# Two-layer transformer-like block on one core: diagonal attention tiles packed two to a bank, and the turned output blocks handled by ScalarE and GpSimd

## What is computed

```python
# first attention: scores plus a slope times the distance
scores = einsum('bhqd,bhkd->bhqk', Q, K) / sqrt(16) + slope * (k - q)
attn   = softmax(where(k <= q, scores, -inf))
out    = einsum('bhqk,bhkd->bqhd', attn, V)
# second attention: rotated q and k, 4 key heads shared by 16 query heads
scores = where(k <= q, einsum('bqhd,bkhd->bhqk', q, k) * scale, min)
out    = einsum('bhqk,bhkd->bqhd', softmax(scores), v)
```

## Time and profile before

| | us |
|---|---|
| median of 3 runs (2500.06 to 2501.35) | 2500.09 |
| the profiled execution | 2502.25 |
| its span, first to last instruction | 2500.4 |
| TensorE busy | 2322.5 (93%) |
| VectorE busy | 1916.5 (77%) |
| ScalarE busy | 1514.3 (61%) |
| GpSimd busy | 583.8 (23%) |

### The profile page before, as it was taken

The page is one execution under the profiler, slowest core; times in us unless marked ns, Lnnn a source line. Parts: engine busy times, 40 slices in busy tenths (PEclk is TensorE's granted clock), DMA queues, the critical chain, the costliest instruction groups (busy, mean ns, idle before and its releaser), DMA issues. The chain is left out here.

```text
span 2500.4 us, 49324 instructions
## 1 busy us (share of the span) xinstructions
PE 2322.5 (93%) x16370; PEld 1302.1 (52%) x16371; DVE 1916.5 (77%) x5054; ACT 1514.3 (61%) x3292; POOL 583.8 (23%) x845
## 2 busy tenths in 40 slices
PE   3599989999999999999999999999998874999997
PEld 2355555444444444444444444444444653788886
DVE  7777658999999999999999999999981663333332
ACT  3133323688888888888888888887886551222221
POOL 6412101121111111211211211111010366333323
PEclk8799996999999999999999999999999986999999
DMA  4167776453443443322332332331032973344443
GB/s 159 64 188 216 209 202 90 82 110 76 77 82 80 75 81 81 61 55 60 62 58 57 61 60 54 61 67 50 25 91 86 301 269 146 71 76 76 78 76 70
DMA packets 168152, 246.51 MB, mean 99 GB/s; under 512 B 52120, under 2 KB 124968, under 8 KB 162100
## 3 DMA queue, kind: packets, MB, share of 16 engines
q0 software_dynamic: 38304, 112.51, 23.9%
q1 hardware_dynamic: 124596, 121.03, 16.5%
q10 hardware_dynamic: 5044, 10.32, 1.4%
HBM read 120.38 MB, written 122.36 MB: 97 GB/s over the span
## 5 line engine op out<-in xcount | busy, mean ns | idle before, releaser
L1404 ACT ACTIVATE a_p<-banks 128x512 f32<-128x512 f32 (+3 forms) x2560 | 1169.6, 542 | 282.1 <-PE banks L1307 174.7
L1451 DVE TENSOR_REDUCE a_mx<-banks 128x1 f32<-128x512 f32 x1536 | 962.3, 683 | 23.8 <-PE banks L1298 21.4
L1368 PE MATMUL banks<-a_p,a_v 128*32 128x512 f32 (+3 forms) x5120 | 601.6, 547 | 1.7 <-ACT a_o L1422 1.7
L1447 DVE CUSTOM_DVE_ANT_0 a_masked<-banks,a_later 128x128 bf16<-128x128 f32 (+3 forms) x1024 | 460.1, 486 | 42.6 <-PE banks L1298 28.8
L1298 PE MATMUL banks<-a_k,a_q 48*128 48x512 f32 (+7 forms) x1600 | 454.5, 428 | 2.9 <-DVE a_mx L1451 1.0
L1307 PE MATMUL banks<-a_q,a_k 50*128 50x512 f32 (+7 forms) x1600 | 433.2, 407 | 1.1
L1298 PEld LDWEIGHTS banks<-a_k,a_q 52*128 52x128 f32 (+1 forms) x1600 | 216.4, 185 | 205.7 <-DVE a_mx L1451 132.5
L1307 PEld LDWEIGHTS banks<-a_q,a_k 54*128 54x128 f32 (+1 forms) x1600 | 216.6, 185 | 137.2 <-ACT a_p L1404 38.3
L1298 PE MATMUL banks<-a_k,q 48*128 48x512 f32 (+7 forms) x896 | 255.0, 434 | 3.1 <-DMA a_k<-aug_rows 1.3
L1307 PE MATMUL banks<-q,a_k 50*128 50x512 f32 (+7 forms) x896 | 236.7, 414 | 0.7 <-DVE a_mx L1447 0.2
L2141 ACT ACTIVATE e_hT<-banks 128x256 fp32r<-128x256 f32 x72 | 27.6, 383 | 309.2 <-PE banks L2067 278.9
(11 more groups left out here) (267 smaller groups left out, 2629.1 us busy)
## 6 DMA issues: line engine op xcount, KB each, us to landing
expert_rows<-a_zeros POOLq DMA_DIRECT2D x132, 258.0 KB, 5.3
a_k<-ka_parts POOLq DMA_DIRECT2D x42, 256.0 KB, 6.3
e_x<-expert_rows SPq DMA_DIRECT2D x72, 129.0 KB, 2.9
expert_rows<-e_y SPq DMA_DIRECT2D x72, 128.0 KB, 2.1
qa_parts<-m_part SPq DMA_DIRECT2D x16, 512.0 KB
ka_parts<-m_part SPq DMA_DIRECT2D x16, 512.0 KB, 4.9
va_tiles<-m_va SPq DMA_DIRECT2D x8, 1024.0 KB, 4.7
qb_parts<-m_part SPq DMA_DIRECT2D x16, 512.0 KB, 4.7
```

Source lines behind the costliest of these rows:

```text
L1368: ins = pe.matmul(ps_o[VW * h:VW * h + VW, c0:QB], v_op[o][:, kt, hk * VW:hk * VW + VW], prob[:, (t * NSC + n * GH + h) % NPB, c0:QB], sta ...
L1404: nc.scalar.activation(prob[:, (t * NSC + n) % NPB, c0:QB], ps[bank][:, c0:QB], ACT.Exp, scale=SCALE).then_inc(s_ex, 1)
L1447: ins = v.tensor_tensor_reduce(masked[:, 2 * (DIAGONAL.index(m) % 2) + j, 0:w], ps[bank][:, 0:w], later[:, WIDE - w:WIDE], 1.0, MASKED, AL ...
L1451: ins = v.tensor_reduce(top, ps[bank][:, 0:w], AX.X, ALU.max)
```

## The change

Diagonal tiles that don't fill a bank share one: of each pair of heads, the tile of 384 columns with that of 128 (`ends`), and the two pairs' tiles of 256 (`middle`). The number and width of the products stays, but for the mask's, which now treat both tiles of a bank at once (moving operand 64 or 2 x 64 columns); VectorE still does one masked maximum for each tile, ScalarE one exponential for each bank. A step has 136 banks of maxima, 136 of scores and 280 in all. A score group of the value product is now a full key tile, `widest`, `ends` (eight products of two records each) or `middle`; there are 36 of them for 40.

The maxima of query blocks 0 and 1 no longer pass through `mx` and the last reduction (DIRECT = 2): block 0's masked maximum is written straight to `row_top`, block 1's takes the maximum of its first key block in `mx` as its starting value through a pointer. `row_top` has two buffers. Blocks 2 and 3 are as before. The scratch `masked` has 2 buffers for 4.

A turned output block is copied by ScalarE from the bank to `t_sb` (272 columns), VectorE takes the reciprocal from there, and GpSimd multiplies (`weigh`, 128 x 256 with the factor broadcast). Both strings are new, with d for ScalarE's copy and a new letter e for reciprocal, product and store. In `ORDER` (312 letters for 348) the e stands directly behind its d for output block 3, 34 places behind it for blocks 0 and 2, and 68 for block 1. In `FIRST_ORDER` the first score of query blocks 0 to 3 stands 3, 3, 10 and 6 places behind the w of its row maxima, for 19, 21, 28 and 29 before. LEAD is 42 (of 68), SLEAD 4. TensorE now waits for the mask `later` too before its first product.

```diff
+def score_groups():
...
+        widest = [[(p, 4 * qb, 0, QB, 0)] for p in range(PAIRS)]
+        ends = [[(p, 4 * qb + 1, P, 3 * P, P), (p, 4 * qb + 3, 3 * P, P, 0)] for p in range(PAIRS)]
+        middle = [[(p, 4 * qb + 2, 2 * P, 2 * P, 2 * P * p) for p in range(PAIRS)]]
...
+            def weigh(t, n):
+
+                pool.wait_ge(s_rc, t * NQB + (n + 1))
+                pool.wait_ge(s_os[n % 2], t * (NQB // 2 * 16) + (n // 2 * 16 + 16))
+                nc.gpsimd.tensor_tensor(o_row[n % 2][:, :, :].rearrange("p j (h c) -> p j h c", h=GH),
+                                        t_sb[n % 2][:, :, :, 0:HD],
+                                        rec[n % 2][:, :, :].unsqueeze(3).to_broadcast([P, 4, GH, HD]), ALU.mult
+                                        ).then_inc(s_or, 1)
...
-            pe.wait_ge(M["s_masks"], 48)
+            pe.wait_ge(M["s_masks"], 64)
...
-                        ins[j] = pe.matmul(outs[j][:, HALF * n:HALF * (n + 1)], steps[n][half, :], fill[half, :],
+                        blocks = outs[j][:, lo:lo + len(at) * apart].rearrange("p (b c) -> p b c", c=apart)
+                        ins[j] = pe.matmul(blocks[:, :, HALF * n:HALF * (n + 1)], steps[n][half, :],
+                                           fill[half, :].unsqueeze(1).to_broadcast([HALF, len(at), HALF]),
...
+                    elif what == "turn copied":
+                        turned = ps[BANKS[t]["turn", n]].rearrange("p (j h c) -> p j h c", j=4, h=GH)
+                        act.wait_ge(s_tt, t * NQB + (n + 1 + TT0))
+                        if t > 0 or n >= 2:
+
+                            act.wait_ge(s_or, t * NQB + (n - 1))
+                        nc.scalar.activation(t_sb[n % 2][:, :, :, :], turned[:, :, :, 0:HD + 1], ACT.Copy).then_inc(s_te, 1)
...
+                for p, qt, k0, w, col in tiles:
+                    top = mx[:, j, p, qt, k0 // WIDE:k0 // WIDE + 1]
+                    if diagonal:
+                        least = mx[:, j, p, qt, 0:1] if qb == 1 else MASKED
+                        if qb < DIRECT:
+                            top = row_top[:, qb % 2, j * PAIRS + p, qt % 4:qt % 4 + 1]
+                        ins = v.tensor_tensor_reduce(masked[:, j, col:col + w], ps[bank][:, col:col + w],
+                                                     later[:, WIDE - w:WIDE], 1.0, least, ALU.add, ALU.max, top)
+                    else:
+                        ins = v.tensor_reduce(top, ps[bank][:, :], AX.X, ALU.max)
...
-                if m == LAST_MAX[qb] and j == 1:
+                if m == LAST_MAX[qb] and j == 1 and qb >= DIRECT:
...
-                        ch.did(v.reciprocal(rec[:, :, :], turned[:, :, :, HD]))
-                        ch.settle()
...
-                        v.tensor_tensor(o_row[n % 2][:, :, :].rearrange("p j (h c) -> p j h c", h=GH),
-                                        turned[:, :, :, 0:HD],
-                                        rec[:, :, :].unsqueeze(3).to_broadcast([P, 4, GH, HD]), ALU.mult
-                                        ).then_inc(s_te, 1)
+                        v.reciprocal(rec[n % 2][:, :, :], t_sb[n % 2][:, :, :, HD]).then_inc(s_rc, 1)
```

More of the change, by code:

```diff
@@ L934 @@
 NPB = 20
[L935 to L960, removed]
+LEAD = 42
+SLEAD = 4
+def score_groups():
+    groups = []
+    for qb in range(NQB):
+        full = [[[(p, kt, 0, QB, 0)] for p in range(PAIRS)] for kt in range(4 * qb)]
+        widest = [[(p, 4 * qb, 0, QB, 0)] for p in range(PAIRS)]
+        ends = [[(p, 4 * qb + 1, P, 3 * P, P), (p, 4 * qb + 3, 3 * P, P, 0)] for p in range(PAIRS)]
+        middle = [[(p, 4 * qb + 2, 2 * P, 2 * P, 2 * P * p) for p in range(PAIRS)]]
+        between = [ends, middle, widest] if qb else [widest, ends, middle]
+        for d, diagonal in enumerate(between):
+            groups += [(qb, False, pairs) for pairs in full[len(full) * d // 3:len(full) * (d + 1) // 3]]
+            groups.append((qb, True, diagonal))
+    return groups
@@ new lines, in max_banks, with full, ends, widest @@
+def max_banks():
+    banks = []
+    for qb in range(NQB):
+        first = 4 * qb * P
+        def full(p, i):
+            return [(qb, False, [(p, 4 * qb + i, k0, WIDE, 0)]) for k0 in range(0, first, WIDE)]
+        def ends(p):
+            return [(qb, True, [(p, 4 * qb + 2, first, 3 * P, P), (p, 4 * qb, first, P, 0)])]
+        def widest(p):
+            return [(qb, True, [(p, 4 * qb + 3, first, WIDE, 0)])]
+        middle = [(qb, True, [(p, 4 * qb + 1, first, 2 * P, 2 * P * p) for p in range(PAIRS)])]
+        banks += full(0, 0) + full(0, 2) + ends(0) + full(0, 1) + full(0, 3) + widest(0)
+        banks += full(1, 1) + middle + full(1, 0) + full(1, 2) + ends(1) + full(1, 3) + widest(1)
+    return banks
@@ new lines @@
+GROUPS, MAXES = score_groups(), max_banks()
+SCORES = [(qb, diagonal, tiles) for qb, diagonal, pairs in GROUPS for tiles in pairs]
+NSP, NMX, NGR = len(SCORES), len(MAXES), len(GROUPS)
+SFIRST = [sum(len(pairs) for of, _, pairs in GROUPS if of < qb) for qb in range(NQB)]
+VFIRST = [sum(of < qb for of, _, _ in GROUPS) for qb in range(NQB)]
+RUN = [g for g in range(NGR) for _ in GROUPS[g][2]]
+PAIR0 = [RUN.index(g) for g in range(NGR)]
+KEYED = [min(m for m in range(NMX) if MAXES[m][2][0][2] >= k0) for k0 in (WIDE, 2 * WIDE)]
@@ L1049, in attention @@
         o_sb = [sb(f"a_o{i}", [P, QB]) for i in range(2)]
-        rec = sb("a_rec", [P, 4, GH])
+        t_sb = [sb(f"a_turned{i}", [P, 4, GH, HD + 1]) for i in range(2)]
+        rec = [sb(f"a_rec{i}", [P, 4, GH]) for i in range(2)]
         o_row = [sb(f"a_orow{i}", [P, 4, GH * HD]) for i in range(2)]
@@ L1242, in step @@
                         parts(t, h)
+                    elif what == "inverse":
+                        weigh(t, h)
                     elif h % 2:
@@ L1266, in _, with mask @@
             pe.sem_inc(s_rt, RT0)
-            pe.sem_inc(s_pv, PV0)
-            pe.wait_ge(M["s_masks"], 48)
-            def mask(outs, steps):
+            pe.wait_ge(M["s_masks"], 64)
+            def mask(outs, tiles, steps):
+                at = [col for _, _, _, _, col in tiles]
+                lo, apart = min(at), abs(at[-1] - at[0]) or P
                 ins = [None, None]
@@ L1339, in step @@
                     elif what == "score":
[L1340 to L1341 removed]
+                        qb, _, tiles = SCORES[n // 2 % NSP]
+                        if n % 2 == 0 and n // 2 % NSP == SFIRST[qb]:
                             pe.wait_ge(s_mr[qb], (t + n // NSC + 1) * NMR)
@@ L1349, in step @@
                             score_half(t + n // NSC, n + 1, second)
-                            at = columns(qb, kt)
-                            for ins in mask([ps[b][:, at:at + P] for b in (bank, second)], after_q):
+                            for ins in mask([ps[b] for b in (bank, second)], tiles, after_q):
                                 ins.then_inc(s_sc, 1)
```

163 lines of the change are left out of this document (83 added, 80 removed).

## The result

The kernel became slower: 2514.59 us, median of 20 executions (2496.63 to 2520.97), against 2502.03 of 20 of the kernel before; ratio 1.0036, interval 1.0023 to 1.005. The forecast was 2453, range 2420 to 2478. The profiled execution took 2516.19 us, with a span of 2514.4.

What follows compares the result with a forecast made beforehand. VectorE, slightly ahead of TensorE and tied to it by 7 banks, was taken as the bound. Steps 1 to 14 at -3.3 us each gave -46, step 0 -1, last step and tail 0: -47, to 2453 us, range 2420 to 2478.

Steps and rivals of the forecast that it cites:

- The step that failed: GpSimd in steps 1 to 14: 3 us of multiplies a step, covered by 2 us to the next queued work; cost nothing.
- packing, row tops, banks, narrow tiles: Steps 1 to 14: direct row tops save 0.7 us a step, fewer banks and fuller tiles 1.2.
- pointer: Block 1's 16 masked maxima a step take their start from SBUF: 0 to 0.06 us each, 0.45 taken.
- turned blocks: Product and a wait leave VectorE, a reciprocal stays: four blocks save 2.3 us a step in steps 1 to 14.
- VectorE's wait for ScalarE's copy: Block 3's reciprocal directly follows its copy, so VectorE waits: +0.45 us a step, 0.2 to 2.
- the tie of the ring: VectorE and TensorE, nearly full, share 7 banks: 4.8 of 93.0 us a step lost, 1.2 recovered, bounds 0 and 3.5.
- The wait for `later`: Ahead of TensorE's first product: moves only a start that VectorE made no use of; 0, bound 1 us.
- The tail: End of attention: last block's copy, GpSimd multiply and two more hand-overs before the final store add 1.0 us.
- Rival 1: Steps 1 to 14: the VectorE-TensorE tie dissolves, 87.5 us a step, -5.5; 2420 us in all; chance 0.17.
- Rival 2: TensorE was the pace, or pointer and copy cost their upper ends: -1.6 us a step, 2477; chance 0.21.
- Rival 3: Pointer counts as second SBUF input, multiplies stop block 1's masked maxima, up to 3.0 us a step: 2496; 0.06 with no gain.
- Rival 4: With 2 scratch buffers, 40 diagonal banks a step may wait: up to 7.2 us, net +3.9 a step, 2555; chance 0.06.

Runs made afterwards that it cites:

- filler run: Kernel after, with five dummy products on TensorE ahead of the late parts of block 3 and the next block 0, from step 1 on: 2494.27 us, ratio 0.9952.
- the two one-block runs: Kernel after, with GpSimd forming only one query block's row-maxima parts early, from step 1 on: block 3's 2491.41 us, the next step's block 0's 2480.76 us.
- parts first: Kernel after, with GpSimd alone forming row-maxima parts directly behind the last maximum needed, ahead of loads, clearings and multiplies: 2448.04 us, ratio 0.9764.
- the old order's: Kernel before, its order and banks kept, with turned blocks copied by ScalarE and multiplied by GpSimd at the old letter, 2 scratch buffers: 2598.35 us, ratio 1.0361.
- block 0's run: Kernel after, with GpSimd forming only the next step's block 0 parts ahead of multiply and clearing, from step 1 on: 2480.76 us, ratio 0.9902.

## Why the prediction was wrong

**The step that failed** is "GpSimd. ... Behind the multiply are queued the parts of the next row maxima and DMA issues, 7 letters (2 us) behind at the nearest, which covers it", costed at nothing. Three things were wrong in it. Distance in letters covers only a duration, and I compared it with the multiply's 0.75 us; but the multiply *waits*, for a reciprocal that stands in VectorE's queue behind maxima (2.22 us ahead of 1422.67). Behind it come not only the parts but a clearing (0.78) or two load issues (0.5 each, 0.59 between). And for block 3 I never looked for what the new string does to the margin from the last maximum to the turn: it is 9 letters with 8 banks, where it was 11 with 11, so loads and clearings that did no harm before now do. What it cost is shown by the edit of one queue, 5.16 us a step in place of nothing.

**The term that was absent** is TensorE's clock. In the earlier trace rows it was 1.00 and I took that as given. The account of the 5.16: waits 38.0 / 14 = 2.7; the rest, 2.45, falls on 99 / 14 = 7.1 us of half clock, 0.34 us lost for each. Other readings give about the same price: steps of 92.5 us (3.4 over 89.1, waits 2.3, half clock 3.4: 1.1 / 3.4 = 0.32), steps of 95.6 (6.5 over, waits 2.9, half clock 10.2: 3.6 / 10.2 = 0.35), and, apart from this trace, the 20 executions of the kernel after, whose times fall by 1.63 us per 0.001 of mean clock, from 2518.64 at 0.939 to 2496.63 at 0.954, where 0.001 of the span is 5.0 us at half clock: 0.33 (whatever else varied with the clock is in it). The filler run gave 0.32, single steps of the two one-block runs 0.27 to 0.39. It is not 0.5; that part of such a stretch is not TensorE's to set would explain it, and is not shown. That the clock has a price of its own is shown by the filler run and by steps with equal stops.

The other terms, measured where nothing waits for parts (steps of 89.11):

| term, a step | forecast | measured |
|---|---|---|
| packing, row tops, banks, narrow tiles | -1.45 with pointer | -2.5 |
| ... idle before narrow tiles | 2.1, of which 1.2 goes | 0.1 left |
| ... pointer | +0.45 | +1.0 (16 x 0.06) |
| turned blocks | -2.3, +0.45 for the copy | -1.8 |
| ... VectorE's wait for ScalarE's copy | +0.45 | none in steps 1 to 14 |
| ... GpSimd's multiply | 0.75 each | 0.62 each |
| GpSimd's queue and the clock | 0 | +5.2 |
| step | -3.3 | +0.9; -4.2 with parts first |

So what was priced for VectorE was right in kind. Offload came to its sum, 1.85, by two errors that cancel (a copy's wait that is not there, a gain 0.5 smaller). Row tops, banks and narrow tiles gave 3.5 before the pointer's 1.0, where I had 1.9 and 0.45: the tie of the ring loosened more than I dared take. The forecast for the kernel with parts first would have missed by 5 us.

**Outside the steps.** *Step 0* was forecast at -1 and came at -0.2, which its spread of 5.6 us hides. *The wait for `later`:* TensorE stood 5.1 us for it, and VectorE began at 371.5 for 372.4 us: nothing lost, as said. *The tail* was forecast at +1.0; all engines in order of time, kernel after, end of the attention (against the earlier trace rows):

```profile
1923.76 0.60 ACT L1483 ACTIVATE a_o<-banks 128x512 f32<-128x512 f32 x1 [1.25 <-PE banks L1418]
...
1925.16 0.40 ACT L1478 ACTIVATE a_turned<-banks 128x272 f32<-128x272 f32 x1 [0.81 <-PE banks L1427]
1925.60 0.25 DVE L1532 RECIPROCAL a_rec<-a_turned 128x16 f32<-128x16 f32 x1 [9.54 <-ACT a_turned L1478]
1925.93 0.62 POOL L1266 TENSOR_TENSOR a_orow<-a_turned,a_rec 128x256 f32<-128x256 f32 x1 [9.16 <-DVE a_rec L1532]
1926.58 0.36 SPq L1220 DMA_DIRECT2D attention_rows<-a_orow  x1
1932.43 0.20 POOL L1711 MEMSET p_ones<- 128x128 f32 x1 [5.88 <-POOLq L1051]
```

Copy to store takes 2.8 us for 2.2, less than the 1.0 more that I priced, and the store lands after 1.9 as it did; but the next stage begins 5.85 us behind its issue, where it was 2.35. It is so with parts first too (8.7 us from copy to next stage, 4.6 before). The runs tell what the 3.5 us go with: from the last store's issue to the next stage it was 5.8 to 5.9 us in all eight kernels in which GpSimd multiplies, the old order's too, and 2.4 in the four in which VectorE does, with the packed banks as without. So they are a price of moving the last block, where GpSimd has its last work just before the stage ends; why it takes 5.88 us from there on no run shows. The tail came at +4.1 for the +1.0 forecast. From copy to copy the last step was 5.0 us shorter (78.9 for 83.9) where I had -1, which pays for the tail; 6.8 us of the 83.9 ran at half clock, none of the 78.9.

**The rivals.** None held. Rival 1 (the tie dissolves, 2420) had 87.5 a step; with parts first the 89.1 lie between it and the forecast's 90.0, and nearer the forecast. Rival 2 (TensorE was the pace, 2477) named the engine that in the end stopped, but for another reason: its cure was not fewer products but an earlier input. Rival 3 (port) cost nothing, but its premise was not tested: none of the 64 multiplies ran at the same time as a masked maximum, with or without pointer; beside them ran only plain maxima. The 256 masked maxima with a pointer lasted 753 ns at most. The Trainium skill, page "SBUF — State Buffer", section "Who interferes with whom", would have a pair with two SBUF inputs block each other for a whole instruction; this trace has no such pair with the multiply. All it offers is one masked maximum of 384 columns with a pointer, at 483.6 us, beside the two small instructions of the parts: 608 ns, where the median is 610. Rival 4 (VectorE waits for itself, 2555) is out as the cause: the idle time is ahead of full banks with TensorE as releaser, and with parts first and the same 2 buffers a step takes 89.1 us. The scratch was not varied by itself. The direction had a chance of 0.06 on a mechanism that did not act; a rival "a small operation on which TensorE waits is queued behind bulk work" was missing, though the earlier trace rows showed its instruction, the parts, in this very queue.

## What to carry to other kernels

An engine with spare time is not a free place for work: its queue is in order, and if a small operation on which the critical engine waits passes through it, each thing placed ahead delays that operation by its duration and by *its own wait*. So list, for every moved instruction, what the engine does behind it and who needs that, and move the small urgent operation to the earliest place where its input exists; here that reorder in one queue turned +0.4% into -2.4%. Where rows show that the clock falls behind a stop of TensorE, charge the stop twice, once for itself and once for the half clock: here 2.7 and 2.45 us of the 5.16.

## What the runs showed of the hardware

- Of the stops of TensorE of 1.3 to 2.6 us in steps 1 to 14 of the kernel after, an otherwise full stage, 20 of 22 were followed by a stretch of 3.4 or 6.8 us at a granted clock of about 0.5, and none of the six of 0.8. In block 0's run, with one stop a step from step 2 on, four of the six of 1.4 us were (steps 8 to 13), and the one of 1.3 was not. With products in place of the stops (the second filler run) steps 2 to 14 had none.
- A microsecond at half clock cost about a third of a microsecond in this stage (0.27 to 0.39 by the readings above); the one stretch of the kernel before, 6.8 us in a step 3.2 us longer than its neighbours, gives 0.47.
- A pointer from SBUF as the start of VectorE's masked maximum costs 0.06 us, at 128 columns (286 to 347 ns) as at 512 (687 to 746).
- GpSimd's multiply of 128 x 256 with a broadcast factor takes 0.62 us, VectorE's out of a bank 0.42.

The fastest version is the kernel after with parts first: 2448.04 us, 2.7% under the kernel after and 2.4% under the one before. Open is why the next stage starts 5.9 us after a last store whose rows GpSimd multiplied, and 2.4 after VectorE's.
